# Four groups' value projection beside the last softmax, both projection weights in one product for the others

## The reference, cut to what matters

```
x = _layernorm(x + _L1_gnn_ref(...))          # x2: end of layer 1
# layer 2, graph attention over E = 512 edges, 4 heads
Xq = x @ W_lin.T
Xv = x @ W_val.T
e  = leaky_relu(Xq[:, src] + Xq[:, dst]) . a + log(adj[src, dst])
attn = softmax of e over the edges with one src
Y  = sum over edges of attn * Xv[:, dst]
x = _layernorm(x + Y @ W_out.T)
```

## Time and profile before

| | |
|---|---|
| median of 3 runs | 1893.49 us (1893.24 to 1894.81) |
| profiled execution | 1891.92 us, its span 1890.1 us |
| granted TensorE clock, mean | 0.981 |
| busy: PE, DVE, ACT, POOL | 1805.4 (96%), 1462.7 (77%), 1097.1 (58%), 576.7 us (31%) |
| projection stage, PE at full clock | from about 1374 to 1489.8 us of the span |
| scores | 1491.5 to 1634.6 us |
| DMA, mean | 38 GB/s |

### The profile page before, as it was taken

The page is one execution under the profiler, slowest core; times in us unless marked ns, Lnnn a source line. Parts: engine busy times, 40 slices in busy tenths (PEclk is TensorE's granted clock), DMA queues, the critical chain, the costliest instruction groups (busy, mean ns, idle before and its releaser), DMA issues. The chain is left out here.

```text
span 1890.1 us, 35902 instructions
## 1 busy us (share of the span) xinstructions
PE 1805.4 (96%) x13479; PEld 1483.3 (78%) x13479; DVE 1462.7 (77%) x3912; ACT 1097.1 (58%) x1721; POOL 576.7 (31%) x1638
## 2 busy tenths in 40 slices
PE   7999999999999999999999999989799899699997
PEld 6777778888899999988887878867599644388875
DVE  7889876566577677878888879878677579798776
ACT  4555565445455455544444447757577588566676
POOL 3454421233234342000000024456644000104655
PEclk9999999999999999999999999989799999899998
DMA  4012010001000000010000025212222000003223
GB/s 136 27 35 68 2 45 1 1 1 45 1 1 1 1 1 1 1 45 1 1 1 1 1 97 152 95 41 94 67 79 68 23 1 1 12 1 96 87 74 108
DMA packets 61689, 71.49 MB, mean 38 GB/s; under 512 B 3782, under 2 KB 55244, under 8 KB 61516
## 3 DMA queue, kind: packets, MB, share of 16 engines
q1 hardware_dynamic: 61516, 69.20, 11.4%
HBM read 44.03 MB, written 25.17 MB: 37 GB/s over the span
## 5 line engine op out<-in xcount | busy, mean ns | idle before, releaser
L2034 ACT ACTIVATE l_gates<-l_acc,l_b 128x512 f32<-128x512 f32 (+1 forms) x408 | 239.9, 620 | 84.6 <-PE l_acc L480 82.6
L478 PE MATMUL l_acc<-l_x_hi,l_w1x_hi 128*128 128x336 f32 (+1 forms) x544 | 188.3, 346 | 1.1 <-ACT l_gates L2034 0.8
L480 PE MATMUL l_acc<-l_x_lo,l_w1x_hi 128*128 128x336 f32 (+1 forms) x544 | 187.6, 345 | 0.0
L479 PE MATMUL l_acc<-l_x_hi,l_w1x_lo 128*128 128x336 f32 (+1 forms) x544 | 187.2, 344 | 0.0
L478 PE MATMUL l_acc<-l_x_hi,l_w0x_hi 128*128 128x512 f32 x464 | 181.9, 392 | 2.7 <-ACT l_gates L2034 2.6
L1923 ACT ACTIVATE l_x_hi<-hT 128x512 fp32r<-128x512 f32 (+1 forms) x112 | 82.4, 786 | 174.7 <-PE l_acc L480 174.7
L479 PE MATMUL l_acc<-l_x_hi,l_w0x_lo 128*128 128x512 f32 x464 | 181.3, 391 | 0.0
L480 PE MATMUL l_acc<-l_x_lo,l_w0x_hi 128*128 128x512 f32 x464 | 181.2, 391 | 0.0
L2044 ACT ACTIVATE l_gates<-l_cell 128x512 f32<-128x512 f32 (+1 forms) x112 | 63.7, 569 | 167.3 <-DVE l_cell L2095 137.6
L249 POOL TENSOR_TENSOR bi_shifted<-bi_shifted 32x126 f32<-32x126 f32 (+61 forms) x62 | 18.0, 290 | 390.7 <-DVE bi_shifted L236 390.7
L1270 ACT ACTIVATE leaky<-sc_g 128x1024 f32<-128x1024 f32 x128 | 121.2, 1032 | 17.2 <-PE sc_g L1391 16.8
(11 more groups left out here) (492 smaller groups left out, 5436.1 us busy)
## 6 DMA issues: line engine op xcount, KB each, us to landing
xin<-in_x_t SPq DMA_DIRECT2D x16, 512.0 KB, 3.6
hidB<-in_x SPq DMA_DIRECT2D x16, 512.0 KB, 5.1
x<-hT SPq DMA_DIRECT2D x16, 512.0 KB, 3.1
hidB<-x SPq DMA_DIRECT2D x16, 512.0 KB, 3.9
x<-hidB SPq DMA_DIRECT2D x16, 512.0 KB, 2.9
attention_residual<-x SPq DMA_DIRECT2D x16, 512.0 KB, 3.9
out_x<-hT SPq DMA_DIRECT2D x16, 512.0 KB, 2.9
l_rawx<-in_wih SPq DMA_DIRECT2D x4, 1024.0 KB, 5.9
```

The source lines that it names most:

```text
L478: t.matmul(out, left[0], right[0], start=start, stop=False)
L479: t.matmul(out, left[1], right[0], start=False, stop=False)
L480: return t.matmul(out, left[0], right[1], start=False, stop=stop)
L2034: i = a.activation(gates[:, j, q, 0:n], acc[:, j, q, 0:n], FUNC[q], bias=b[:, o:o + 1])
```

## The change

- In groups 0 to 11 a tile of xt meets both weights in one product of 512 columns; ps_qv holds, in each of its four banks, the queries and values of one tile. ACT drains two tiles (queries, then values) and DVE the other two; both wait for the store of x2 of this group. wqv is laid out with both weights side by side.
- In groups 12 to 15 (`later.FIRST` = 12) only queries are made, in alternating halves of the PSUM.
- xt of groups 12, 13 and 14 is stored to DRAM by SP, behind x2 of groups 14 and 15 and at the end, each store waiting for the one before; ACT waits for that of group 12 before it writes xt of group 14 in its place. xt of group 15 goes into slots 12 and 13 of hT, the value weights (copied by POOL) into slot 14.
- In the second block POOL reads xt of 12, 13, 14 back into slots 4 to 9 of xq when their stacks are built. Behind the last dots PE makes the values of groups 15, 12, 13 and 14 in the three buffers of the gather, and ACT drains them: the first before the last exponent, two before and one after the last weights.

The diff, cut to its core:

```diff
+class LaterValues:
...
+    FIRST = GROUPS - 4
+    SLOT = C * GROUP
...
+        self.stay, self.back = values, queries
+        self.dram = [[nc.dram_tensor(f"x2t_later{g}{n}", [P, self.SLOT], F32, kind="Internal").ap() for n in range(2)]
+                     for g in range(self.FIRST, GROUPS - 1)]
+        half = self.SLOT // 2
+        self.weights = [self.slot(values, GROUPS - 2)[:, n * half:(n + 1) * half].rearrange("p (c d) -> p c d", c=C) for n in range(2)]
+        self.last = [self.by_feature(self.slot(values, self.FIRST + n)) for n in range(2)]
+        self.again = [2 * (g - self.FIRST) + self.AT for g in range(self.FIRST, GROUPS - 1)]
+
+    AT = 4
...
+    def rows(self, g):
+        if g == GROUPS - 1:
+            return self.last
+        return [self.by_feature(self.slot(self.back, self.again[g - self.FIRST] + n)) for n in range(2)]
...
-        ps_q, ps_v = (ps_hid[:, C * n:C * n + C].rearrange("p c (h d) -> p (c h) d", d=D) for n in range(2))
+        ps_qv = ps_hid[:, :, :].rearrange("p r (v d) -> p r v d", d=D)
+        ps_q = [ps_hid[:, C * n:C * n + C].rearrange("p c (h d) -> p (c h) d", d=D) for n in range(2)]
+        BY_SCALAR, BY_VECTOR = slice(0, TILES // 2), slice(TILES // 2, TILES)
...
+        def xt_of(g):
+            return later.last if g == LAST else [z[:, :, :] for z in xt[g % 2]]
...
+            def put_rows_by(g):
+                sp.wait_ge(xl, g + 1)
+                if g > later.FIRST:
+                    sp.wait_ge(put_by, (g - later.FIRST) * 32)
+                for n in range(2):
+                    sp.dma_start(later.by_feature(later.dram[g - later.FIRST][n]), xt[g % 2][n][:, :, :].bitcast(F32)).then_inc(put_by, 16)
...
                 sp.dma_start(x2v[g], rows(hidB, g)).then_inc(stored2[g % SEMS], 16)
+                if g - 2 >= later.FIRST:
+                    put_rows_by(g - 2)
+            put_rows_by(LAST - 1)
+            sp.wait_ge(put_by, (LAST - later.FIRST) * 32)
...
+            pool.wait_ge(o_scaled, LAST * C)
+            for n in range(2):
+                p.tensor_copy(later.weights[n], wqv[n][:, :, 1]).then_inc(moved, 1)
+            pool.wait_ge(moved, 2)
...
-                a.activation(xt[g % 2][0][:, :, :], ps_mix[:, :, :], ACT.Copy).then_inc(xh, 1)
+                if later.FIRST <= g - 2 < LAST - 2:
+                    act.wait_ge(put_by, (g - 1 - later.FIRST) * 32)
+                a.activation(xt_of(g)[0], ps_mix[:, :, :], ACT.Copy).then_inc(xh, 1)
...
                 act.wait_ge(stored2[g % SEMS], (g // SEMS + 1) * 16)
-                a.activation(rows(hidB, g), ps_q, ACT.Copy).then_inc(qd, 1)
+                if g >= later.FIRST:
+                    a.activation(rows(hidB, g), ps_q[g % 2], ACT.Copy).then_inc(qd, 1)
+                    return
+                a.activation(rows(hidB, g)[:, BY_SCALAR], ps_qv[:, BY_SCALAR, 0], ACT.Copy).then_inc(qd, 1)
+                a.activation(rows(hT, g)[:, BY_SCALAR], ps_qv[:, BY_SCALAR, 1], ACT.Copy).then_inc(qd, 1)
...
             def values(g):
                 dve.wait_ge(qv, g + 1)
-                v.tensor_copy(rows(hT, g), ps_v).then_inc(vd, 1)
+                dve.wait_ge(stored2[g % SEMS], (g // SEMS + 1) * 16)
+                v.tensor_copy(rows(hidB, g)[:, BY_VECTOR], ps_qv[:, BY_VECTOR, 0]).then_inc(vd, 1)
+                v.tensor_copy(rows(hT, g)[:, BY_VECTOR], ps_qv[:, BY_VECTOR, 1]).then_inc(vd, 1)
...
-                if g:
+                if 0 < g <= later.FIRST:
                     values(g - 1)
...
             dve.wait_ge(qd, 2)
+            dve.wait_ge(vd, 2)
             queries_ready(dve)
-            values(LAST)
...
-                if g:
-                    pe.wait_ge(qd, g)
-                    pe.wait_ge(vd, g)
-                else:
+                if g > later.FIRST + 1:
+                    pe.wait_ge(qd, later.FIRST + g - 1)
+                elif 0 < g <= later.FIRST:
+                    pe.wait_ge(qd, 2 * g)
+                    pe.wait_ge(vd, 2 * g)
+                elif not g:
                     pe.wait_ge(out, GROUPS * C)
...
-                    for n, dst in enumerate((ps_q, ps_v)):
-                        for k in range(C):
-                            i = product(t, dst[:, r], (xt[g % 2][0][:, k, f], xt[g % 2][1][:, k, f]),
-                                        (wqv[0][:, n, k], wqv[1][:, n, k]), k == 0, k == C - 1)
+                    hi, lo = xt_of(g)
+                    for k in range(C):
+                        dst, w = (ps_qv[:, r], [z[:, k] for z in wqv]) if g < later.FIRST else (ps_q[g % 2][:, r], [z[:, k, 0] for z in wqv])
+                        i = product(t, dst, (hi[:, k, f], lo[:, k, f]), w, k == 0, k == C - 1)
...
+        LATER = [GROUPS - 1] + list(range(later.FIRST, GROUPS - 1))
+        ps_v = [z[:, :, :].rearrange("p c (h d) -> p (c h) d", d=D) for z in ps_g]
...
+            for g in LATER[1:]:
+                at = later.again[g - later.FIRST]
+                pool.wait_ge(stacked, 8 * (at + 1) + 8)
+                for n in range(2):
+                    nc.gpsimd.dma_start(later.rows(g)[n], later.by_feature(later.dram[g - later.FIRST][n])).then_inc(rows_in[g - later.FIRST], 16)
...
+            def values(n):
+                act.wait_ge(valued, n + 1)
+                a.activation(group_of(hT, LATER[n]).rearrange("p c (h d) -> p (c h) d", d=D), ps_v[n % GATHERS], ACT.Copy).then_inc(
+                    values_copied, 1)
+            values(0)
             exponent(QUARTS - 1)
             weights_ready(act)
+            values(1)
+            values(2)
             for n, part in enumerate(COLUMN_HALVES):
                 weights_hi(QUARTS - 1, n, part)
+            values(3)
...
             dots(B // 4 - 1)
+            for n, g in enumerate(LATER):
+                if n:
+                    pe.wait_ge(rows_in[n - 1], 32)
+                if n >= GATHERS:
+                    pe.wait_ge(values_copied, n - GATHERS + 1)
+                hi, lo = later.rows(g)
+                for r in range(TILES):
+                    f = slice(r * P, (r + 1) * P)
+                    for k in range(C):
+                        i = product(t, ps_v[n % GATHERS][:, r], (hi[:, k, f], lo[:, k, f]), [z[:, k] for z in later.weights], k == 0, k == C - 1)
+                i.then_inc(valued, 1)
             turn(QUARTS - 1, 0, range(EC // 2))
             turn(QUARTS - 1, 1, range(EC // 2, EC))
...
+            pe.wait_ge(scored["values"], scored["later"] - 1)
             t.transpose(ps_z, ev.signed[:, :], c["ident"][0:N, 0:N]).then_inc(z_done, 1)
             pe.wait_ge(scored["high"], QUARTS + 1)
             pe.wait_ge(scored["low"], QUARTS + 1)
+            pe.wait_ge(scored["values"], scored["later"])
```

More of the change, by code:

```diff
@@ L2180, in on_tensor @@
         conv[4](pe)
-    return m, spectral, scores, place, hidB, (on_sync, on_gpsimd, on_scalar, on_vector, on_tensor)
+    return m, spectral, scores, place, later, hidB, (on_sync, on_gpsimd, on_scalar, on_vector, on_tensor)
 class RowNorm:
@@ L2613, in network @@
         with ExitStack() as wide:
-            m, spectral, scores, place, hidB, layers = first_layers(nc, layer_sem, wide, c, bi, ev, hT, a, x1, x2, par1, par2)
+            m, spectral, scores, place, later, hidB, layers = first_layers(nc, layer_sem, wide, c, bi, ev, hT, values, a, x1, x2, par1, par2)
             xq = hidB[:, :, :, :].rearrange("p g c n -> p (g c n)")
```

29 lines of the change are left out of this document (20 added, 9 removed).

## The result

| kernel | median of the runs, us | runs | profiled execution, us (span) |
|---|---|---|---|
| before, beside it | 1893.37 (1893.08 to 1894.81) | 4 | 1891.92 (1890.1) |
| changed | 1881.83 (1881.15 to 1882.7) | 4 | 1882.7 (1880.6) |

The ratio is 0.9946, with a 95% interval of 0.9933 to 0.996: faster, by 11.5 us between the medians and 9.2 between the two profiled executions. The forecast was 1884.3.

A forecast was written before the change was run, and what follows sets the result against it. PE was taken as the bound (busy 96% of the span), with waits for drains and a low clock after rests. Terms -0.8 - 6.2 - 2.2 = -9.2 us from the median 1893.49 gave 1884.3, range 1880.5 to 1889.0.

The forecast's parts named there:

- Wide products: Projection groups 0 to 11: 24 products of 512 columns replace 48 of 256; -0.8 us, bounds -1.15 and +0.5.
- the drain: PSUM drain in groups 0 to 11: two halves last 0.07 to 0.15 us more; 0 to 0.1 us shows.
- The tail: End of the projection stage: values of groups 12 to 15 leave, SP's stores end the block; -6.2 us.
- its hops: Serial store steps in the tail: SP's stores land in 6.0, 6.0 and 4.5 us.
- the moving: Data transfer within each tail store: 512 KB takes 1.5 us at 346 GB/s, plus 1.4 us fixed.
- rival B: Tail: stores quicker than the profile row, compute chain ends the block; at the most down to 1879.8 us, chance 0.12.
- GpSimd's two copies: Tail: copying the V weights takes under 2.8 us, covered by 11 us; uncovered, the 2.8 would count in full.
- The score stage: Second block: GpSimd's six 512 KB reloads into Xq have 50 us of cover; cost none.
- The softmax: Gap of the last softmax: moved values keep the clock up for the pair products; -2.2 us, bounds -2.4 and +2.8.
- C: Tail: each store hop costs like the 5.9 us issue, so the tail gives -2.0; 1888.5 us, chance 0.15.
- D: Projection groups: split drains show, 0.3 us a group, +2.2 instead of -0.8; 1887.3 us, chance 0.08.
- E: Tail: serial store hops last so long that the block ends later than before; 1896.8 us at 170 GB/s, chance 0.03.

The follow-up runs named there:

- wide_only: The kernel before with wide products and split drains in all sixteen groups and no values moved: 1888.71 us, ratio 0.9987.
- move_only: The changed kernel with groups 0 to 11 taking their two weights one after the other again, with the old drains: 1882.94 us, ratio 0.996.
- no_serial: The changed kernel without SP's waits between one group's xt stores and the next: 1881.41 us, ratio 0.9944.
- fill_tail: early_stores with 27 products that feed nothing in PE's rest of 3.4 us in the tail: 1879.06 us, ratio 0.993.
- after_again: The changed kernel run again unchanged: 1881.01 us, ratio 0.996.
- early_stores: The changed kernel with xt of groups 12 and 13 stored ahead of x2 of groups 14 and 15, not behind: 1878.4 us, ratio 0.9936.
- mid: early_stores with group 13's values made in PE's rest in the tail, leaving three groups of values for the last softmax's gap: 1879.43 us, ratio 0.9933.

## Why the prediction was right, and where its sizes were off

**Wide products, -0.8 forecast, -1.05 measured.** The step that was mis-sized is the drain: 0.35 us of it were taken off for eleven groups, 0.03 each, and groups 0.07 us shorter were forecast. They are 0.10 shorter (7.34 us against 7.44), nearly the 0.106 of the pitches, so that what the drain shows after a group's last product is all but given back at its first, and wide_only's 1.50 over fifteen groups repeats it. The halves on DVE lasted 1.28 us, just under the 1.3 to 1.38 forecast. The step from the drain's end to the next product, which the prediction put at about 0.1 of 0.16 us, is 0.15 in both kernels (in that of before also where PE stands and waits, 1476.40 to 1476.55), so the drain was on the path already and little of it could hide.

**The tail, -6.2 forecast, -7.3, -6.4 and -6.6 measured in three profiles.** The chain is the one laid out: scaling of 14, stores of 12, ACT's wait, scaling of 15, stores of 15 and 13, stores of 14, block 2. Counted from the ends of the scalings, and the last one to block 2, its hops were forecast at 6.1, 6.1 and 5.0 us (4.6 to the landing and 0.4 behind it). They took 1469.26 - 1463.60 = 5.66, 6.02 (6.94 and 6.83 in the repeats) and 4.45 (3.95 to the landing and 0.50 behind it): together 1.1 less, the whole of what the tail gained beyond its forecast. The mis-sized term is the moving: 1.53 us for half a megabyte, since "a DMA share of 1.03 leaves nothing". That window was on a store in pieces of 1 KB, and its rate holds for such a store here too (341 GB/s, above). The xt stores move the same in 2.75 / 2 = 1.38 us. The prediction had this in its rival B ("they have 4 KB pieces, the row's 1 KB") and set it aside. Against it stands the second hop in two of three profiles, longer by 0.8 to 0.9 us where transfers of instructions fell amid the stores and one DMA engine came late, which the prediction did not have at all; with it the tail is -6.4 and -6.6, near the forecast for two reasons that offset each other. The clock in the tail was low for 3.4 us instead of about 5, and compute ended 0.6 us ahead of the stores instead of 0.4. GpSimd's two copies took 0.61 us each, within the bound of 2.8 and hidden as said.

For a megabyte in one go the prediction set 6.15 us, a figure of the Trainium skill, page "DMA: Bandwidth & Descriptors", section Bandwidth, beside its own 4.5. The page measured loads into SBUF that GpSimd issued. Here two halves of a megabyte, stores that SP sends one behind the other, land 3.95 us after the first issue, and their data moves for 2.75 us of it. The measurement decides for the row of this kernel.

**The score stage, 0 forecast, -0.01 measured.** The last reload is issued at 1566.05 and lands at 1571.28, 54 us before the values begin.

**The softmax, -2.2 forecast, -2.25 measured.** The first pair product starts 0.08 us later after the dots ("at most 0.1"), and at full clock. That the clock stays up is likely, not certain: it did in five profiles with four groups of values in the gap and fell in two (move_only, no_serial: 79.5 us, so 0.7 of the 2.25 remained). What it is held against is no more certain: the stretch was 80.26 in the profile of before and 79.23 in wide_only's. The remaining rest of 1.4 us is enough for it. The prediction had this case as a bound at 0.

**What it did not have:** the clock's falls elsewhere. The +1.33 us at the spectral stage in the first profile is one, and where the opening's low clock ends is another. They hit both kernels: near 1305, ahead of all that was changed, the clock fell for 3.4 us in the profiles of before, the changed kernel, wide_only and fill_tail and in no other. The six runs of after_again alone span 6.6 us. The forecast of 1884.3 was the median of before less 9.2. Its sum matches the two profiled executions (9.2), and that is luck in part: the three terms forecast at 9.2 came to 10.6, and the spectral stage's 1.3 took most of the rest back. Meanwhile the medians differed by 11.5 here and by 8.5 when the changed kernel ran again. The terms that moved from 9.2 are known by size: tail -1.1 to -0.2, wide products -0.25, spectral start +1.3 or 0. What part of the remaining difference between 11.5 and 8.5 lies in which stage of the unprofiled executions was not settled.

**The rivals.** B (stores quicker, compute ends the block) came by half: the stores were quicker, but compute did not end the block in the changed kernel; in early_stores and move_only it does, and in no_serial both end together to 0.1. C (5.9 us hops) came in the second hop alone, by 0.8 to 0.9 us, in two profiles of three, and for a reason of its own. D and E did not.

## What to carry to other kernels

Work that is moved has two prices: the place that it leaves and the place where it comes to lie. Here a gap of 10 us was worth 2.3 us to whatever fills it, idle products included, and mid shows the reverse, the same gain lost when a quarter of the filling was taken out. Put a store behind the event that makes its data ready, not behind the next store in program order: two moved lines gave 2 to 3 us, more than the wide products. And when whole times scatter by 3 to 4 us, compare landmarks: the tails of the five kernels with that rest filled agreed to 0.01 us, while the kernel before, unchanged, had medians from 1889.51 to 1893.37. Where clock or DMA enter, a landmark scatters too (the changed kernel's tail from 21.21 to 22.10), and one profile of each kernel is not enough.

## What the runs showed of the hardware that I had not expected

- The granted clock after a short rest of PE is not the same from one execution to the next. A rest of 2.26 us at the same place of the same kernel left it at 1.00 once and dropped it to 0.50 for 3.4 us once, at 1.33 us.
- It can fall when PE is busy again: after the rest of 4.7 us in the tail it was 1.00 through the rest and fell in the window in which PE resumed; in no_serial it fell in the window from 1638, in which the pair products began.
- The full DMA moved 347 GB/s in one microsecond and 412 to 417 in others, at a share of 1.01 to 1.05: the first in pieces of 1 KB, the others in pieces of 4 KB.
- Transfers of instructions go through the same 16 DMA engines. One of 16 KB took 0.9 to 1.1 us, and where it fell amid the store of x2 this store of 512 KB landed after 4.3 to 4.7 us and not 3.0; in after_again one engine was still busy 1.2 us after the others.
